# Product keys: seven lags in place of four, rounds written out, two PSUM copies on ScalarE, GpSimd's sums behind another wait

## The reference, cut to the phase

```python
q = (hidden_states @ Wq).reshape(b, t, 2, H, RET // 2)          # H = 4, RET = 128
sim = jnp.einsum('btphn,hkpn->pbthk', q, keys)                  # 64 keys a half
sc, ix = jax.lax.top_k(sim, 8)
all_sc = (sx[..., :, None] + sy[..., None, :])                  # 64 candidates
scores, pk = jax.lax.top_k(all_sc, 8)
w = jnp.einsum('btd,bthkd->bthk', hidden_states, down_embed[idx])
w = jax.nn.silu(w) * jax.nn.softmax(scores, axis=-1)
experts_states = jnp.einsum('bthk,bthkd->btd', w, up_embed[idx])
mlp = jax.nn.silu(hidden_states @ Wg + bg) * (hidden_states @ Wu + bu) @ Wd + bd
return mlp + experts_states
```

## Time and profile before

| what | value |
|---|---|
| median of 3 runs | 2956.55 us (2956.48 to 2957.0) |
| the profiled execution: its own time | 2959.04 us |
| its span, first to last instruction | 2957.3 us |
| mean granted TensorE clock | 0.92 |
| PE busy over the span | 2472.5 us (84%) |
| DVE busy | 1543.0 us (52%) |
| ACT busy | 1323.0 us (45%) |
| POOL busy | 973.2 us (33%) |

### The profile page before, as it was taken

How to read it: one execution, slowest core, us unless ns; L and a number is a source line. 1 busy time by engine, 2 the same in 40 slices (tenths; PEclk the granted TensorE clock), 3 DMA queues, 4 the chain that set the end, 5 groups by cost and what they waited for, 6 DMA issues and landing times. The chain is left out here.

```text
span 2957.3 us, 55320 instructions
## 1 busy us (share of the span) xinstructions
PE 2472.5 (84%) x16024; PEld 2024.4 (68%) x16024; DVE 1543.0 (52%) x4339; ACT 1323.0 (45%) x3147; POOL 973.2 (33%) x1298
## 2 busy tenths in 40 slices
PE   6899999988797853986899999988699997863895
PEld 3577777767686752983567777767578776762885
DVE  4466666544214345116666666644688885425111
ACT  3466667653231421324656667753344442242221
POOL 0233444411105555545532333311333330544002
PEclk9999999998897976998999999999899998985998
DMA  8121222202564363521122222210100001253684
GB/s 276 57 72 65 85 76 71 86 21 108 196 240 122 111 203 117 178 64 60 52 82 74 64 86 75 65 48 23 60 1 0 0 0 59 85 187 131 240 308 164
DMA packets 150859, 296.59 MB, mean 100 GB/s; under 512 B 25158, under 2 KB 110406, under 8 KB 144560
## 3 DMA queue, kind: packets, MB, share of 16 engines
q1 hardware_dynamic: 138416, 262.92, 26.4%
q0 software_dynamic: 12288, 31.83, 3.5%
HBM read 240.25 MB, written 64.56 MB: 103 GB/s over the span
## 5 line engine op out<-in xcount | busy, mean ns | idle before, releaser
L797 DVE CUSTOM_DVE_ANT_0 prob_l<-ps_l,bias_l,nsn 128x1024 f32<-128x1024 f32 (+3 forms) x256 | 276.7, 1081 | 108.2 <-DVEq L796 62.1
L797 DVE CUSTOM_DVE_ANT_0 cur_sb<-ps_h,bias_s,nsn 128x128 f32<-128x128 f32 (+3 forms) x256 | 139.8, 546 | 238.0 <-DVEq L796 237.8
L725 PE MATMUL ps_l<-khi,stage 128*128 128x512 f32 (+3 forms) x512 | 257.1, 502 | 0.0
L872 ACT ACTIVATE prob_l<-prob_l,nmax 128x1024 f32<-128x1024 f32 (+3 forms) x256 | 252.1, 985 | 2.5 <-DVE nmax L797 2.2
L731 PE MATMUL ps_pt<-ident_sb,prob_l 128*128 128x128 f32 x1664 | 236.7, 277 | 6.1 <-ACT cur_sb L856 2.1
L856 ACT ACTIVATE cur_sb<-ps_pt 128x128 f32<-128x128 f32 (+3 forms) x256 | 110.8, 433 | 264.4 <-PE ps_pt L731 264.4
L690 POOL TENSOR_TENSOR stage<-qo,stage 64x256 fp32r<-64x256 f32 x256 | 198.2, 774 | 47.8 <-POOLq L689 47.8
L731 PEld LDWEIGHTS ps_pt<-ident_sb,prob_l 128*128 128x128 f32 x1664 | 185.8, 141 | 37.0 <-ACT cur_sb L856 15.9
L2271 POOL TENSOR_TENSOR ss<-simx,sim 128x4096 f32<-128x4096 f32 x16 | 113.4, 7085 | 242.6 <-DVE simx L2420 242.6
L681 POOL COPY nsn<-nsn 128x4 f32 (+1 forms) x128 | 25.6, 200 | 505.1 <-DVE diff L814 378.9
L1657 ACT ACTIVATE hT<-ps_h,mlp_ws 128x128 f32<-128x128 f32 x312 | 89.1, 369 | 224.3 <-PE ps_h L1630 224.3
(11 more groups left out here) (338 smaller groups left out, 6102.1 us busy)
## 6 DMA issues: line engine op xcount, KB each, us to landing
mlp_ws<-in_L_ffn_experts_dram SPq DMA_DIRECT2D x39, 2052.0 KB, 7.4
xs<-slot_rows SPq DMA_DIRECT2D x156, 128.0 KB, 2.1
slot_outputs<-ys SPq DMA_DIRECT2D x156, 128.0 KB, 1.9
slot_rows<-zero_sb SPq DMA_DIRECT2D x1, 16384.0 KB, 52.2
bias_l<-in_fside_16xSxS_dram SPq DMA_DIRECT2D x16, 512.0 KB, 3.4
mlp_w<-in_L_ffn_experts_dram SPq DMA_DIRECT2D x8, 1024.0 KB, 7.5
bias_by_partition<-bias_table SPq DMA_DIRECT2D x16, 512.0 KB, 4.1
bias_l<-bias_by_partition SPq DMA_DIRECT2D x16, 512.0 KB, 3.3
```

Of the source, the lines that this page charges most:

```text
L725: ins = pe.matmul(out, stage[:, b, s, x.h % 2, x.h // 2, :], att[part][:, b * S + lo:b * S + hi], start=False, stop=part == "klo", skip_gr ...
L797: dve.tensor_tensor_reduce(out=spans(x, prob), in0=scored(x), in1=spans(x, bias), scale=-1.0, scalar=nsn[:, b, s, h:h + 1], op0=ALU.add, o ...
L872: act.activation(prob[x.s][:, x.h, 0:x.W], prob[x.s][:, x.h, 0:x.W], ACT.Exp, bias=nmax[:, x.b, x.s, x.h:x.h + 1], scale=-1.0, accum_out=r ...
```

## The change

The lists of all engines are written anew with lags from 0 to 6 (seven in place of four), and `unrolled` writes out all rounds, so there is no loop and every count is a constant:

```diff
-            pipeline(gp, NT, 4, (0, stage), (1, sums))
+            unrolled(gp, NT, 2, (3, sums))
-            pipeline(pe, NT, 4, (0, transposes), (3, outputs), (0, queries), (2, retrieval), (0, similarities), (2, hidden))
+            unrolled(pe, NT, 6, (4, first_gate_up), (5, turned), (5, outputs), (4, last_gate_up), (0, transposes), (1, queries),
+                     (4, retrieval), (1, similarities))
-            pipeline(act, NT, 4, (0, transposed), (1, exponentials), (0, queries), (2, hidden))
+            unrolled(act, NT, 6, (4, first_gates), (5, turned), (3, exponentials), (4, last_gates), (0, transposed), (1, queries),
+                     (4, retrieved), (1, similarities))
-            pipeline(dve, NT, 4, (2, all_coefficients), (3, outputs), (2, weighed), (0, search), (2, first_hidden),
-                     (0, search_sums), (2, last_hidden))
+            unrolled(dve, NT, 6, (5, weighed), (6, outputs), (2, search), (4, first_hidden), (2, search_sums), (4, all_coefficients),
+                     (4, last_hidden))
```

The copy of x into `xs` goes; PE transposes `cur` itself:

```diff
-            def stage(t, u):
-
-                gp.wait_ge(pe_x.sem, pe_x.after("xT", t - 2))
-                gp.tensor_copy(xs[:, u % 2, :], at(c["cur"], t)).then_inc(gp_x.sem, 1)
...
-                    ins = pe.transpose(ps_x[:, k * P:(k + 1) * P], xs[:, u % 2, k * P:(k + 1) * P], c["ident"][:])
+                    ins = pe.transpose(ps_x[:, k * P:(k + 1) * P], c["cur"][:, t, k * P:(k + 1) * P], c["ident"][:])
```

`sums` keeps its three waits and its one instruction, with more buffers:

```diff
-                gp.tensor_tensor(ss[:, u % 2].rearrange("p h (a b) -> p h a b", b=NK),
-                                 simx[:].unsqueeze(3).to_broadcast([P, HR, NA, NK]),
-                                 sim[:, 1].unsqueeze(2).to_broadcast([P, HR, NA, NK]), ALU.add).then_inc(gp_a.sem, 1)
+                gp.tensor_tensor(ss[:, t % 2].rearrange("p h (a b) -> p h a b", b=NK),
+                                 simx[:, t % 2].unsqueeze(3).to_broadcast([P, HR, NA, NK]),
+                                 sim[:, t % 3, 1].unsqueeze(2).to_broadcast([P, HR, NA, NK]), ALU.add).then_inc(gp_a.sem, 1)
```

Two copies out of PSUM move from VectorE to ScalarE: `sim`, and VectorE's half of `gT`:

```diff
+            def similarities(t, u):
+                act.wait_ge(pe_s.sem, pe_s.after("sim", t))
+
+                act.wait_ge(gp_a.sem, gp_a.after("ss", t - 3))
+                act.wait_ge(dve_a.sem, dve_a.after("simx", t - 3))
+                act.activation(sim[:, t % 3].rearrange("p q h n -> p (q h n)"), ps_s[:], ACT.Copy).then_inc(act_s.sem, 1)
...
-                act.activation(gT[:, 0:BANK], ps_w[:, 0:BANK], ACT.Copy).then_inc(act_b.sem, 1)
+                act.activation(gT[:], ps_w[:], ACT.Copy).then_inc(act_t.sem, 1)
...
-                dve.tensor_copy(sim[:].rearrange("p q h n -> p (q h n)"), ps_s[:]).then_inc(dve_a.sem, 1)
...
-                dve.tensor_copy(gT[:, BANK:], ps_w[:, BANK:]).then_inc(dve_b.sem, 1)
```

On VectorE the waits of search, search_sums and hidden become:

```diff
-                dve.wait_ge(pe_s.sem, pe_s.after("sim", t))
-
-                dve.wait_ge(gp_a.sem, gp_a.after("ss", t - 1))
+                dve.wait_ge(act_s.sem, act_s.after("sim", t))
+                dve.wait_ge(dve_a.sem, dve_a.after("t8", t - 1))
...
+                dve.wait_ge(gp_a.sem, gp_a.after("ss", t - 2))
...
-                    dve.wait_ge(pe_y.sem, pe_y.after("y", t - 1))
+                    dve.wait_ge(pe_y.sem, pe_y.after("y", t - 2))
```

TensorE's hidden stage is cut in two. `gate_up(t, u, q)` keeps its wait, and the transposes of `gm` are a stage of their own, `turned`:

```diff
+                pe.wait_ge(dve_h.sem, dve_h.after(f"h{(q + 2) % 4}", t - 1 if q < 2 else t))
...
+            def first_gate_up(t, u):
+                gate_up(t, u, 0)
+                gate_up(t, u, 1)
+
+            def last_gate_up(t, u):
+                gate_up(t, u, 2)
+                gate_up(t, u, 3)
```

More of the change, by code:

```diff
@@ L2224, in product_key_phase @@
         pe_s = ph.steps("sim")
[L2225 removed]
+        act_s = ph.steps("sim")
+        dve_a = ph.steps("s8 top s8x simx cand ready t8")
         gp_a = ph.steps("ss")
@@ L2305, in similarities, with gate_up @@
                 ins.then_inc(pe_s.sem, 1)
+            def gate_up(t, u, q):
+                if t == 0 and q == 0:
+                    pe.wait_ge(weights, 16 * len(second))
+                pe.wait_ge(dve_h.sem, dve_h.after(f"h{(q + 2) % 4}", t - 1 if q < 2 else t))
+                for j, ww in enumerate((wg, wu)):
+                    for f in range(2):
+                        fc = 2 * q + f
+                        for k in range(KD):
+                            ins = pe.matmul(ps_gu[:, q % 2, (2 * j + f) * P:(2 * j + f + 1) * P],
+                                            ww[:, k, fc * P:(fc + 1) * P], xT[:, u, k, :], start=(k == 0), stop=(k == KD - 1))
+                ins.then_inc(pe_g.sem, 1)
+            def first_gate_up(t, u):
[4 more added lines that the diff above has]
+                gate_up(t, u, 3)
             def retrieval(t, u):
-                pe.wait_ge(weights, 16 * len(second))
-                pe.wait_ge(act_b.sem, act_b.after("gT", t - 1))
-                pe.wait_ge(dve_b.sem, dve_b.after("gT", t - 1))
+                pe.wait_ge(act_t.sem, act_t.after("gT", t - 1))
                 for lo in range(0, NE, BANK):
@@ new lines, in exponentials, with gate @@
+            def exponentials(t, u):
+                act.wait_ge(dve_a.sem, dve_a.after("t8", t))
+                act.wait_ge(dve_m.sem, dve_m.after("sum8", t - 2))
+                act.activation(e8[:, t % 2], t8[:, t % 3], ACT.Exp).then_inc(act_e.sem, 1)
+                act.wait_ge(gp_a.sem, gp_a.after("ss", t))
+                act.wait_ge(dve_m.sem, dve_m.after(f"kept{HR - 1}", t - 2))
+                act.activation(es[:, t % 2], ss[:, t % 2], ACT.Exp).then_inc(act_e.sem, 1)
+            def gate(t, u, q):
+                if t == 0 and q == 0:
+                    act.wait_ge(weights, 16 * len(second))
+                act.wait_ge(pe_g.sem, pe_g.after(f"gu{q}", t))
+                act.wait_ge(dve_h.sem, dve_h.after(f"h{q}", t - 1))
+                for f in range(2):
+                    fc = 2 * q + f
+                    ins = act.activation(sg[:, fc * P:(fc + 1) * P], ps_gu[:, q % 2, f * P:(f + 1) * P], ACT.Silu,
+                                         bias=bg[:, fc:fc + 1])
+                ins.then_inc(act_g.sem, 1)
@@ new lines, in first_gates, with last_gates, retrieved, turned @@
+            def first_gates(t, u):
+                gate(t, u, 0)
+                gate(t, u, 1)
+            def last_gates(t, u):
+                gate(t, u, 2)
+                gate(t, u, 3)
+            def retrieved(t, u):
+                act.wait_ge(pe_w.sem, pe_w.after("w", t))
+                act.wait_ge(dve_g.sem, dve_g.after("gm", t - 1))
+                act.activation(sw[:], ps_w[:], ACT.Silu).then_inc(act_w.sem, 1)
+            def turned(t, u):
+                act.wait_ge(pe_t.sem, pe_t.after("gT", t))
```

142 lines of the change are left out of this document (55 added, 87 removed).

## The result

The changed kernel takes 2991.72 us (median of 4 runs, 2988.83 to 2992.24) against 2956.78 for the kernel before beside it, a ratio of 1.0114 with a 95% interval of 1.0097 to 1.0132: 34.9 us slower. The forecast was 2996, slower. The profiled execution took 2991.91 us, its span is 2990.2, the granted clock 0.915.

What follows compares the result with a forecast made beforehand. PE was taken as near the bound, DVE close behind (21.77 and 20.22 of 23.55 us a round). 4.7 + 399.0 - 361.9 - 2.1 = +39.7 us took the span from 2957.3 to 2997.0; median forecast 2996, range 2964 to 3012.

Steps and rivals of the forecast that it cites:

- POOL's place: POOL's sum starts at the end of the coefficients, behind kept3; nothing covers it on DVE: stall 6.9 us a round.
- DVE's chain and the wait: DVE's own round 18.12 us; first_hidden's wait for PE's gates 0.6, 2.3 or 3.6 us, middle taken: round 27.3.
- Rival A: PE's clock does not fall after its idle: round 25.6 us, 2972 in all; chance 0.12.
- Rival B: POOL's sum partly covered by DVE's work: stall 5.2 us, round 23.3, faster at 2940; chance 0.11.
- Rival C: Nothing on DVE held up for long, PE becomes the bound: round 21.9 us, 2921; chance 0.05.
- Fill: Start of the phase up to coefficients(0), with more DVE work and gate matmuls ahead: +4.7 us, bounds 3 and 9.
- Coefficients (0) to (15): 14 rounds of 27.3 us, less 1.5 for the missing search, plus a last round of 18.3: 399.0, against 361.9 before.
- Drain: From coefficients(15) to the end: 25.4 us in place of 27.5, with weights and hidden halves already further on.
- The sum: All terms of the product-keys phase added up: +39.7 us.
- ACT's copies: ACT takes over the copies of sim and all of gT: 14 of 27 us even at 1 us each, costing nothing.
- The order of the loads: Order of the weight loads: all eight are waited for together, so it costs nothing.
- POOL's xs copy: POOL's copy of xs goes; it was hidden, so no effect was counted.

Runs made afterwards that it cites:

- the filler: Changed kernel with 8 matmuls of 256 columns into unread PSUM columns in PE's idle time: 2979.06 us, ratio 1.0076.
- the run without reads: Changed kernel with POOL filling the same columns with a constant in place of the sums, all waits kept: 2905.52 us, ratio 0.9836.
- the run by heads: Changed kernel with POOL's sum as four instructions, one a head, each waiting for its own kept: 2988.84 us, ratio 1.0110.

## Why the prediction was right

By its own steps, in the profiled executions:

- *POOL's place*: forecast behind kept3, with its turn as co3 ends. So it is. Stall forecast 6.9 us a round on rest; rest takes 7.01 in place of 0.155, so 6.86.
- *DVE's chain and the wait*: 18.12 us and a wait of 2.3, of three values 0.6, 2.3 and 3.6. The waits are 0.70 + 1.44 = 2.1. The round is 27.21 us, forecast 27.3. That the middle value held rested on one idle of 1.82 and one of 4.28 us; the idle was 4.06, and it took the shorter of the two costs, so this choice was nearer to luck than the rest. Rival A, without the fall of the clock, was forecast at 25.6 a round, and the filler shows 25.59.
- *Rival B's reason*, that POOL's sum is partly covered once a piece of DVE's work stands before rest, holds as arithmetic (with the rest chain last the round is 18.1 plus the 5.9 that is left of the stall, 24.04), but is not what the change does: `rest`, at four columns, is held up for all of the sum.
- *Rival C's floor* was PE at 21.8 to 21.9 us a round; the run without reads shows 21.26. The forecast does not use it, but C would have been some 9 us faster than its 2921.
- *Fill*: +4.7 forecast; 2091.96 - 2055.03 = 36.93 after against 32.63 before, +4.3. *Coefficients (0) to (15)*: 399.0 forecast, 2490.32 - 2091.96 = 398.36; the last of these rounds, 2471.97 to 2490.32, took 18.35 where 18.3 had been chosen between 15.5 and 21.8 without a row for it. *Drain*: 25.4 forecast, 2516.86 - 2490.32 = 26.5; gm of the last tile waited 2.08 us for sw, and the matmuls behind a 2.37 us idle were slow for a while. The rows are from the timeline of the changed kernel, the first and the last coefficients and the last tile:

```profile
2091.96 0.17 DVE L2457 TENSOR_REDUCE sum<-e 128x4 f32<-128x32 f32 x1
...
2490.32 0.18 DVE L2457 TENSOR_REDUCE sum<-e 128x4 f32<-128x32 f32 x1
...
2504.99 1.22 DVE L2511 TENSOR_TENSOR gm<-sw,co 128x1024 f32<-128x1024 f32 x1 [2.08 <-ACT sw L2406]
...
2506.26 1.44 PE L2336 MATMUL ps_w<-ident_sb,gm 128*128 128x128 f32 x8 [2.37 <-DVE gm L2511]
```

- *The sum*: +39.7 forecast for the phase, +39.8 measured. That it is this close owes something to luck: the parts are off by -0.4, -0.6 and +1.1 us and nearly cancel. The medians differ by 34.9. The profiled spans differ by 39.8 - 4.8 ahead of the phase - 2.1 behind it = 32.9, and the profiled execution of the kernel before lay 2.3 us above its median, that of the changed one 0.2. So, as far as these two executions tell, the 4.3 us between the measured median and 2996 lie in code that the change does not touch; whether they are chance is not shown.
- Of the steps costed at nothing, ACT's copies are borne out: ACT has 12.23 of 27.21 us. The order of the loads and POOL's xs copy were not varied in any run, so that they cost nothing is not shown by itself.

The Trainium skill's rule ("SBUF — State Buffer", section "Who interferes with whom") was cited for two SBUF inputs against a GpSimd operation that reads. The runs agree: 7.01 us for four columns with the reading sum beside them, 0.15 with the writing fill, and `co3`, issued ahead of POOL, kept its 1.28 us while POOL waited.

## What to carry to other kernels

Before POOL work is moved in a kernel, write down what DVE does in the microseconds behind its new start: here reads from PSUM (1.12 us for four hidden halves), maxima (1.10) and reductions (in the kernel before `sum8` kept its 0.17 us inside the sum) cover it, the first operation with two SBUF inputs pays for the rest of it, at four columns as at 1024, and the first `co`, a TENSOR_SCALAR with one, is no cover either. Look for it in the durations of one line (a median or a maximum far above the minimum), since the waits view does not show it. And when a stage is moved on one engine, follow the ring of waits through the lists of the others before counting the gain.

## What the runs showed that I had not expected

- Which of POOL and DVE goes first can't be read from their starts when these are within 0.1 us. With the whole sum, co3 was issued 0.10 us ahead of POOL and went first (1.28 us). In the run by heads co was issued 0.05 us ahead of POOL's quarter and still went second: 3.02 us, with POOL at 1.90.
- A coverage of 1.03 us moved the round by 3.2 us (27.21 to 24.04): 1.03 of stall, and 2.1 of waits behind gates that PE could now start under the stall, at full clock.
- One float32 matmul of 256 columns has two records of about 0.22 us (16 of them 7.07 us). The kernel before shows it already: the eight matmuls of `up` are x16 there, in 3.62 us.
- A DVE operation with one SBUF input, the first `co`, is held up by POOL's fill, which reads nothing (1.25 us in place of 0.75), and holds up POOL's quarter (2.38 in place of 1.90). So "two SBUF inputs against a read" is not the whole list of what excludes each other.
